# Inverse deviations of the routed tokens: square root and reciprocal against logarithm and exponential

## The chip, the cores and the metric

One core of one Trainium2 chip runs the whole kernel. The metric is the device time of one execution in microseconds (us), given as the median of three runs. The engines are PE (TensorE), ACT (ScalarE), DVE (VectorE), POOL (GpSimd) and SP (the engine that issues most transfers).

## The reference, cut to what matters

3125 nodes with 256 features pass through a graph layer (53125 edges), a linear attention layer, and then a mixture of experts: 8 experts, 2 per token. The change touches only the layer norm ahead of the experts and what is handed on from it.

```python
def _layernorm(x, axis=-1, eps=1e-05):
    m = jnp.mean(x, axis=axis, keepdims=True)
    v = jnp.var(x, axis=axis, keepdims=True)
    return (x - m) / jnp.sqrt(v + eps)

xn = _layernorm(x)
x = x + gnn(xn, src, dst) + mix(xn)
x = x + ffn(_layernorm(x)[None])[0]     # tokens = _layernorm(x)

# in ffn, for each token:
probs = softmax(tokens @ router_w.T)
rw, re = top_k(probs, 2); rw = rw / rw.sum(-1)
out = tokens
for e in range(8):
    h = gelu(tokens @ w1[e] + b1[e]); y = h @ w2[e] + b2[e]
    out = out + combine[:, e:e + 1] * y
```

The kernel sends only the normalized token through the experts. So that the un-normalized x can be added at the end, each token's row also carries its mean (column MEAN) and one plus its deviation (column SPAN): x + tokens = tokens * (deviation + 1) + mean.

## The kernel before, in words

The 3125 nodes are 25 tiles of 125 rows. The kernel runs in three stages. In the first (to about 262 us of the profiled span) nodes are normalized, the attention is computed, and edges are counted into adjacency blocks that PE multiplies. In the second, which I call routing, the tiles are taken in six groups `ROUT` of 2, 5, 5, 5, 5 and 3 tiles. In the third (from about 332 us) 62 chunks of 128 rows go through the experts' two matrix products.

The change lies in routing. Each engine has its own program, written out by hand, and semaphores order them. For a group g the steps are:

- PE `graph3(g)` (L1423) makes the last graph layer's output of the group.
- DVE `add_graph(g)` adds it to x (L1038), takes moments (L1045) and aggregates them (L1048), which leaves mean and variance in `rows[..., MEAN:SPAN+1]` and raises `var2_done`.
- ACT `token_scale(g)` (L668 to L677) waits for that, writes the square root of variance plus eps to `std2` (L673), and then overwrites SPAN with deviation plus one (L676).
- DVE `scale(g)` makes the reciprocal `rstd2` (L1057) and `shift2` = -mean * rstd2 (L1058).
- ACT `normalize_tokens(g)` (L683) applies scale and shift, one instruction per tile, and raises `tk_done` for each.
- PE `transpose_tokens(g)` (L1437) waits for `tk_done` of the whole group. ACT `copy_tokens(g)` (L693, L695) copies the transposed tokens out of the banks. PE `logits(g)` (L1448) multiplies them by the router's weights.
- DVE `choose(g)` (L1065 to L1083) takes the two best experts, ACT takes an exponential of the difference of their logits (L707), PE `positions(g)` (L1460, L1462) counts places in the experts' lists, and DVE `weigh(g)` (L1092 to L1103) makes weights and slots.
- POOL sends the group's tiles to their slots (L559), after `tk_done`, `span_done` and `slot_done`.

The groups are overlapped by the order of each program. ACT's loop for g is: `normalize_tokens(g+1)`, the exponential of g, `copy_tokens(g+1)`, `token_scale(g+2)`. DVE's is: `scale(g+1)`, `choose(g)`, `add_graph(g+2)`, `weigh(g)`. PE's loop, with the filler products `keep_clock` (L1194) that do no work but keep PE busy, is:

```python
            for g in range(NR):
                if g + 2 < NR:
                    graph3(g + 2)
                if g + 1 < NR:
                    pe.wait_ge(tkT_done, copies_to(g + 1))
                    keep_clock(m0, 8)
                    transpose_tokens(g + 1)
                positions(g)
                if g + 1 < NR:
                    pe.wait_ge(lg_read, g + 1)
                    keep_clock(lg_ps, 3)
                    logits(g + 1)
```

After the last group DVE works out the table of chunks (L1118 to L1153), and SP then loads the chunks of the third stage.

ACT evaluates its functions from tables. An ACT_TABLE_LOAD stands in its stream, under the line of the function that needs it, wherever the active table lacks that function.

Of the kernel before, what the change touches and what calls it, by code (L numbers as in the profile page):

```python
# [9 lines left out]
ACT = mybir.ActivationFunctionType  # L10
# [4 lines left out]
TP = 125  # L15
NT = N // TP
J = 5
# [12 lines left out]
TOKEN, NEXT, W_LOW, W_HIGH, MEAN, SPAN = range(D, D + 6)  # L30
# [11 lines left out]
ROUT = [(0, 2), (2, 7), (7, 12), (12, 17), (17, 22), (22, 25)]  # L42
NR = len(ROUT)
# [14 lines left out]
def build(nc, a, out):  # L58
# [4 lines left out]
    with ExitStack() as ctx:  # L63
        def sb(name, shape, dt=F32):
            return ctx.enter_context(nc.sbuf_tensor(name, shape, dt))

        def sem(name):
            return ctx.enter_context(nc.semaphore(name))
# [14 lines left out]
        class Region:  # L83
# [15 lines left out]
        rows = sb("rows", [P, NT, ROW])  # L99
# [92 lines left out]
        ones = sb("ones", [TP, P])  # L192
# [7 lines left out]
        epsc = sb("epsc", [TP, 1])  # L200
# [41 lines left out]
        qn = sb("qn", [P, 2, 2 * TP])  # L242

        stats2 = sb("stats2", [TP, 2, J, 6])
        std2 = sb("std2", [TP, 2, J])
        rstd2 = sb("rstd2", [TP, 2, J])
        shift2 = sb("shift2", [TP, 2, J])
        lg = sb("lg", [TP, J, NX])
# [46 lines left out]
        h1_done, h1_dve, g2_ready, h2_act, h2_dve = map(sem, ("h1_done", "h1_dve", "g2_ready", "h2_act", "h2_dve"))  # L295
        w_in, b2_in, b2_step, b2_done, rows_set, null_set, nulls_stored = map(sem, (
            "w_in", "b2_in", "b2_step", "b2_done", "rows_set", "null_set", "nulls_stored"))
        g3_ready, x2_done, stats2_done, var2_done, std2_done, shift2_done, tk_done = map(sem, (
            "g3_ready", "x2_done", "stats2_done", "var2_done", "std2_done", "shift2_done", "tk_done"))
        t3_ready, tkT_done, lg_ready, lg_read, diff_done, ex_done, oh_done, pos_ready, pos_read = map(sem, (  # L300
            "t3_ready", "tkT_done", "lg_ready", "lg_read", "diff_done", "ex_done", "oh_done", "pos_ready", "pos_read"))
        slot_done, cum_done, table_done = map(sem, (
# [1 line left out]
        span_done, top_done, slot_known = sem("span_done"), sem("top_done"), sem("slot_known")  # L304
# [291 lines left out]
        def _(act):  # L596
# [43 lines left out]
            for t in range(NT):  # L640
                if t in (1, 8):
                    lo, hi = (J, 3 * J) if t == 1 else (3 * J, NT)
# [25 lines left out]
            def token_scale(g):  # L668
                lo, hi = ROUT[g]
                act.wait_ge(var2_done, g + 1)  # L670
                if g >= 2:
                    act.wait_ge(shift2_done, g - 1)
                nc.scalar.activation(std2[:, g % 2, 0:hi - lo], rows[0:TP, lo:hi, SPAN], ACT.Sqrt, bias=epsc[:]  # L673
                                     ).then_inc(std2_done, 1)
                act.wait_ge(std2_done, g + 1)
                nc.scalar.activation(rows[0:TP, lo:hi, SPAN], std2[:, g % 2, 0:hi - lo], ACT.Identity,  # L676
                                     bias=ones[:, 0:1]).then_inc(span_done, 1)  # L677

            def normalize_tokens(g):
                lo, hi = ROUT[g]  # L680
# [5 lines left out]
            def copy_tokens(g):  # L686
# [7 lines left out]
                if n == J:  # L694
                    nc.scalar.copy(tkT[:, g % 2, :, 4 * TP:5 * TP], h0[:, 0:CB].rearrange("p (k n) -> p k n", k=2)  # L695
                                   ).then_inc(tkT_done, 1)

            token_scale(0)
            normalize_tokens(0)
            copy_tokens(0)  # L700
            token_scale(1)
            for g in range(NR):
                n = ROUT[g][1] - ROUT[g][0]
# [41 lines left out]
        def _(dve):  # L745
            step = [0]

            def link(ins):
                step[0] += 1
                ins.then_inc(dve_step, 1)  # L750
                dve.wait_ge(dve_step, step[0])
# [274 lines left out]
            def chain(ins):  # L1026
                link(ins)

            def add_graph(g):
                lo, hi = ROUT[g]  # L1030
                if g >= 3:
                    dve.wait_ge(tk_done, ROUT[g - 3][1])
                dve.wait_ge(g3_ready, hi)
                for j in range(min(3, hi - lo)):
                    both = hi - lo > j + 3
                    end = j + 4 if both else j + 1
                    got = (y0, y1, spare)[j][0:TP, 0:(1 + both) * D].rearrange("p (j d) -> p j d", d=D)
                    nc.vector.scalar_tensor_tensor(x2[:, g % 3, j:end:3, :], got, 0.0, xb[:, lo + j:lo + end:3, :],  # L1038
                                                   ALU.max, ALU.add).then_inc(x2_done, 1 + both)
                known = lo  # L1040
                for t in sorted(range(lo, hi), key=lambda t: ((t - lo) % 3, t)):
                    if t - lo < 3:
                        known += 2 if t + 3 < hi else 1
                        dve.wait_ge(x2_done, known)
                    nc.vector.bn_stats(stats2[:, g % 2, t - lo, :], x2[:, g % 3, t - lo, :]).then_inc(stats2_done, 1)  # L1045
                dve.wait_ge(stats2_done, hi)
                for j in range(hi - lo):
                    last = nc.vector.bn_aggr(rows[0:TP, lo + j, MEAN:SPAN + 1], stats2[:, g % 2, j, :])  # L1048
                last.then_inc(var2_done, 1)

            def scale(g):
                lo, hi = ROUT[g]
                n = hi - lo
                dve.wait_ge(std2_done, g + 1)
                if g >= 2:
                    dve.wait_ge(tk_done, ROUT[g - 2][1])
                chain(nc.vector.reciprocal(rstd2[:, g % 2, 0:n], std2[:, g % 2, 0:n]))  # L1057
                nc.vector.scalar_tensor_tensor(shift2[:, g % 2, 0:n], rows[0:TP, lo:hi, MEAN], -1.0, rstd2[:, g % 2, 0:n],  # L1058
                                               ALU.mult, ALU.mult).then_inc(shift2_done, 1)

            def choose(g):
                lo, hi = ROUT[g]
                n = hi - lo
                dve.wait_ge(lg_ready, g + 1)
                nc.vector.tensor_copy(lg[:, 0:n, :].rearrange("p j x -> p (j x)"), lg_ps[0:TP, 0:n * NX]  # L1065
                                      ).then_inc(lg_read, 1)
                dve.wait_ge(lg_read, g + 1)
                for j in range(n):
                    last = nc.vector.max(top[:, j, :], lg[:, j, :])
                chain(last)  # L1070
                for j in range(n):
                    last = nc.vector.max_index(top_at[:, j, :], top[:, j, :], lg[:, j, :])
                last.then_inc(top_done, 1)
                nc.vector.tensor_tensor(ex[:, 0:n], top[:, 0:n, 1], top[:, 0:n, 0], ALU.subtract).then_inc(diff_done, 1)
                dve.wait_ge(top_done, g + 1)
                for r2, (order, pick) in enumerate(((ALU.is_lt, ALU.min), (ALU.is_gt, ALU.max))):
                    nc.vector.tensor_tensor(first[:, 0:n, r2], top_at[:, 0:n, 0], top_at[:, 0:n, 1], order)
                    last = nc.vector.tensor_tensor(role[:, 0:n, r2], top_at[:, 0:n, 0], top_at[:, 0:n, 1], pick)
                chain(last)
                for r2 in range(2):  # L1080
                    last = nc.vector.tensor_tensor(oh[:, lo:hi, r2, :], iota_x[:, 0:n, :],
                                                   role[:, 0:n, r2:r2 + 1].to_broadcast([TP, n, NX]), ALU.is_equal)
                last.then_inc(oh_done, 1)  # L1083
# [4 lines left out]
            def weigh(g):  # L1088
                lo, hi = ROUT[g]
                n = hi - lo  # L1090
                dve.wait_ge(ex_done, g + 1)
                nc.vector.tensor_tensor(first[:, 0:n, :], first[:, 0:n, :], of_both(ex, n), ALU.max)  # L1092
                chain(nc.vector.tensor_scalar(exs[:, 0:n], ex[:, 0:n], 1.0, None, ALU.add))
                chain(nc.vector.reciprocal(exs[:, 0:n], exs[:, 0:n]))
                nc.vector.tensor_tensor(rows[0:TP, lo:hi, W_LOW:W_HIGH + 1], first[:, 0:n, :], of_both(exs, n), ALU.mult)
                dve.wait_ge(pos_ready, g + 1)
                nc.vector.tensor_tensor(place[:, 0:n, :], pos_from(lo, hi).rearrange("p (j n) -> p j n", n=2 * NX),
                                        oh[:, lo:hi].rearrange("p j r x -> p j (r x)"), ALU.mult).then_inc(pos_read, 1)
                dve.wait_ge(pos_read, g + 1)
                nc.vector.tensor_reduce(slot_f[:, 0:n], place[:, 0:n, 0:NX], AX_X, ALU.add).then_inc(slot_known, 1)  # L1100
                nc.vector.tensor_reduce(rows[0:TP, lo:hi, NEXT], place[:, 0:n, NX:2 * NX], AX_X, ALU.add)
                dve.wait_ge(slot_known, g + 1)
                nc.vector.tensor_copy(slot_i[0:TP, lo:hi, 0], slot_f[:, 0:n]).then_inc(slot_done, 1)  # L1103
# [2 lines left out]
            nc.vector.tensor_scalar(cum[:], base[:], 1.0 / TP, None, ALU.mult).then_inc(cum_done, 1)  # L1106
            add_graph(0)
            scale(0)
            add_graph(1)
            for g in range(NR):  # L1110
                if g + 1 < NR:
                    scale(g + 1)
                choose(g)
                if g + 2 < NR:
                    add_graph(g + 2)
                weigh(g)
# [442 lines left out]
```

## Time and profile before

| | us |
|---|---|
| median of three runs | 474.47 |
| lowest, highest run | 474.03, 477.58 |
| the profiled execution's own time | 479.72 |
| its span, first to last instruction | 478.0 |
| first stage, to | about 262 |
| routing, from and to | about 262 to 332 |
| third stage, from | about 332 |
| PE, DVE, ACT, POOL busy in the span | 435.7, 312.7, 283.2, 175.2 |

The profile is of one execution, 5.25 us longer than the median of the runs. All rows come from it. Their times are counted from the first instruction.

### The profile page before, as it was taken

Reading aid. Unit: us, or ns where it says so; the run is one execution under the profiler, and the core shown is the slowest. Engines: PE = TensorE matmul, PEld = TensorE weight load, DVE = VectorE, ACT = ScalarE, POOL = GpSimd, SP = SyncE. Lnnn points to the kernel's source line nnn. Section 1 sums busy time; section 2 is a strip of 40 time slices with the busy share of each in tenths; the row PEclk is TensorE's granted clock in tenths of the full one; section 3 lists DMA queues with packets and bytes.
Section 4 is the critical chain, followed back from the end, with each engine's and each line's share of the span. In section 5 each row is a group of like instructions: output and inputs, shape, how many; then the busy total and the mean of one; then the engine's idle time right before and its main releaser. Section 6 shows DMA issues by size and latency. Waiting matters only on the chain.

```text
span 478.0 us, 9967 instructions
## 1 busy us (share of the span) xinstructions
PE 435.7 (91%) x3245; PEld 324.2 (68%) x3254; DVE 312.7 (65%) x860; ACT 283.2 (59%) x630; POOL 175.2 (37%) x236
## 2 busy tenths in 40 slices
PE   1899899989999999999998989877899999999990
PEld 0687687866666666555665656553899999889890
DVE  3687959867777777777751787638466666666660
ACT  1657554766767767677772686751676776444440
POOL 5045686454111111111110014455244454544442
PEclk9899999999999999999999979787999999999996
DMA  8827111936789799877776001112466565566640
GB/s 213 182 63 239 41 27 25 331 70 122 119 161 161 150 181 184 183 145 138 142 122 123 1 25 58 57 67 90 115 196 193 175 186 160 152 190 171 186 132 2
DMA packets 111458, 63.05 MB, mean 132 GB/s; under 512 B 87753, under 2 KB 101970, under 8 KB 111406
## 3 DMA queue, kind: packets, MB, share of 16 engines
q1 hardware_dynamic: 104222, 47.11, 44.3%
q0 software_dynamic: 6368, 14.44, 8.9%
q10 hardware_dynamic: 816, 0.85, 0.7%
q8 instruction: 27, 0.44, 0.4%
q14 instruction: 25, 0.20, 0.1%
HBM read 22.96 MB, written 21.44 MB: 93 GB/s over the span
## 4 chain that ended last, share of the span: by engine, by line
PE 71%; DMA 7%; DVE 6%; ACT 6%; issue 3%; POOL 2%; SPq 1%; another core or an unknown queue 1%; POOLq 0%; DVEq 0%; ACTq 0%
PE bank L1300 12%; PE bank L1505 10%; PE bank L1516 10%; PE bank L1251 9%; PE bank L1331 4%; PE bank L1218 4%; PE bank L1227 4%; DMA region_a<-region_a 3%; PE bank L1494 3%; PE bank L1234 3%; DMA rows<-in_x 2%; PE bank L1194 2%; PE bank L1448 2%; PE bank L1311 2%; ACT rows L683 1%
## 5 line engine op out<-in xcount | busy, mean ns | idle before, releaser
L636 ACT CAST region_a<-bank 128x500 bf16<-128x500 f32 (+1 forms) x175 | 112.1, 667 | 46.2 <-PE bank L1251 42.0
L1300 PE MATMUL bank<-region_a,region_z 125*64 125x500 bf16 (+1 forms) x525 | 69.8, 361 | 2.5 <-DMA region_a<-region_a 2.5
L1251 PEld LDWEIGHTS bank<-region_a 128*128 128x128 bf16 x625 | 41.2, 101 | 42.7 <-issue 31.0
L1251 PE MATMUL bank<-region_a 128*128 128x125 bf16 x625 | 64.8, 220 | 1.7 <-ACT region_a L636 1.4
L1505 PE MATMUL bank<-region_a,region_c 128*128 128x128 f32 x496 | 65.8, 275 | 0.3 <-issue 0.3
L1516 PE MATMUL bank<-region_c,region_a 128*128 128x256 f32 x248 | 63.7, 379 | 0.0
L1505 PEld LDWEIGHTS bank<-region_a,region_c 128*128 128x128 f32 x496 | 60.2, 191 | 0.9 <-issue 0.5
L725 ACT ACTIVATE region_a<-bank,region_c 128x128 f32<-128x128 f32 x124 | 38.9, 365 | 33.7 <-PE bank L1505 33.2
L530 POOL COPY wide<-den 125x256 f32<-125x256 f32 x25 | 12.9, 514 | 119.5 <-DVE den L948 119.5
L1163 DVE COPY region_c<-region_w 128x1026 f32 x62 | 43.2, 697 | 16.2 <-issue 15.3
L572 POOL DMA_INDIRECT xs_next<-region_a x31 | 31.4, 1014 | 43.2 <-DVE region_a L1174 42.5
L887 DVE TENSOR_TENSOR region_a<-iota,locs 128x3200 bf16<-128x3200 bf16 x25 | 45.9, 1835 | 0.0
L1516 PEld LDWEIGHTS bank<-region_c,region_a 128*128 128x128 f32 x248 | 42.3, 190 | 4.0
L881 DVE TENSOR_TENSOR region_a<-iota,keys 128x3150 bf16<-128x3150 bf16 x25 | 44.8, 1790 | 0.0
L578 POOL DMA_INDIRECT out<-region_a x31 | 32.0, 1034 | 32.9 <-DVE region_a L1174 31.0
L559 POOL DMA_INDIRECT xs<-rows,slot_i x25 | 24.5, 979 | 51.1 <-DVE slot_i L1103 45.0
L717 ACT COPY region_a<-bank 128x256 f32<-128x256 f32 x62 | 23.1, 373 | 30.2 <-PE bank L1494 23.2
L1300 PEld LDWEIGHTS bank<-region_a,region_z 125*64 125x64 bf16 x525 | 24.4, 108 | 21.4 <-DMA region_a<-region_a 3.0
L1218 PE MATMUL bank<-wzkv,region_a 128*125 128x320 f32 x100 | 32.4, 447 | 0.0
L1171 DVE CAST region_a<-region_a 128x1 int32<-128x1 f32 x62 | 9.5, 154 | 33.9 <-PE bank L1516 29.2
L1194 PE MATMUL bank<-zeros,ones 128*128 128x512 bf16 x98 | 29.4, 443 | 1.5 <-issue 1.1
L1227 PEld LDWEIGHTS bank<-region_a,wq 128*128 128x128 f32 x200 | 27.9, 202 | 4.4 <-issue 0.6
(219 smaller groups left out, 756.1 us busy)
## 6 DMA issues: line engine op xcount, KB each, us to landing
region_a<-xs_next SPq DMA_DIRECT2D x31, 259.0 KB
region_w<-in_w SPq DMA_DIRECT2D x4, 1024.0 KB, 9.7
region_a<-xs SPq DMA_DIRECT2D x31, 131.0 KB
rows<-in_x SPq DMA_DIRECT2D x5, 560.0 KB
xs_next<-null SPq DMA_DIRECT2D x8, 259.0 KB, 2.7
xs_next<-null SPq DMA_DIRECT2D x1, 1554.0 KB, 10.7
xs<-null SPq DMA_DIRECT2D x8, 131.0 KB, 2.3
xs<-null SPq DMA_DIRECT2D x1, 786.0 KB, 7.2
```

The costliest lines, as they stand in the source:

```text
L636: nc.scalar.copy(to, count_bank(n)[:, 0:w * TP].rearrange("p (c t u) -> p c t u", c=w, t=NT)).then_inc(adj_done, 1)
L725: last = nc.scalar.activation(hT[:, c % 2, f * P:(f + 1) * P], hid_ps[c % 2][:, f * P:(f + 1) * P], ACT.Gelu, bias=wc[:, c % 3, 4 * D + f: ...
L881: nc.vector.tensor_tensor(koh[:, t % 2, :, :].rearrange("p c (m u) -> p c m u", u=2), counting(KW), columns(keys, t, KW), ALU.is_equal).th ...
L887: nc.vector.tensor_tensor(loh[:, t % 2, :, :].rearrange("p c (m u) -> p c m u", u=2), counting(P), columns(locs, t, P), ALU.is_equal).then ...
L1163: nc.vector.tensor_copy(wc[:, c % 3, :].rearrange("p (a f) -> p a f", a=1), w_all[:, bass.ds(e, 1), :])
L1194: nc.tensor.matmul(ps[:], ones16[:], zeros[:], start=True, stop=True)
L1218: last = nc.tensor.matmul((y0, y1)[s][0:TP, 0:H1 + D], xnT[:, s, k, :], wzkv[:, k, 0:H1 + D], start=(k == 0), stop=(k == 1))
L1227: last = nc.tensor.matmul((h0, h1)[s][:, c * TP:(c + 1) * TP], wq[:, k, c * P:(c + 1) * P], xnT[:, s, k, :], start=(k == 0), stop=(k == 1))
L1251: last = nc.tensor.matmul(count_bank(n)[:, (c - lo) * TP:(c - lo + 1) * TP], loh[:, t % 2, c, :], koh[:, t % 2, c, 0:TP], start=True, stop ...
L1300: last = nc.tensor.matmul(block_out(b), zparts[:, t, part, :], adjT[0:TP, t % 2, lo:hi, 0:TP], start=False, stop=False, skip_group_check=True)
L1505: last = nc.tensor.matmul(hid_ps[c % 2][:, f * P:(f + 1) * P], wc[:, c % 3, k * D + f * P:k * D + (f + 1) * P], xT[:, c % 2, k * P:(k + 1) ...
L1516: last = nc.tensor.matmul(y_ps[c % 2][:, 0:D], hT[:, c % 2, f * P:(f + 1) * P], wc[:, c % 3, (2 + f) * D:(3 + f) * D], start=False, stop=( ...
```

## The change

ACT takes the logarithm of variance plus eps (into a new tile `log2`), and from it the exponential of -0.5 times that, which is the inverse deviation `rstd2` itself. DVE no longer makes `rstd2` in `scale(g)`. ACT no longer writes SPAN. A new DVE step `restore_scale(g)` takes the reciprocal of `rstd2`, which is the deviation, and writes it plus one to SPAN. It runs right after `scale(0)` for group 0 and after `choose(g-1)` for the others. The waits that protect the buffers follow.

```diff
@@ ACT
             def token_scale(g):
                 lo, hi = ROUT[g]
                 act.wait_ge(var2_done, g + 1)
+                nc.scalar.activation(log2[:, g % 2, 0:hi - lo], rows[0:TP, lo:hi, SPAN], ACT.Ln, bias=epsc[:]
+                                     ).then_inc(log2_done, 1)
+                act.wait_ge(log2_done, g + 1)
                 if g >= 2:
-                    act.wait_ge(shift2_done, g - 1)
-                nc.scalar.activation(std2[:, g % 2, 0:hi - lo], rows[0:TP, lo:hi, SPAN], ACT.Sqrt, bias=epsc[:]
-                                     ).then_inc(std2_done, 1)
-                act.wait_ge(std2_done, g + 1)
-                nc.scalar.activation(rows[0:TP, lo:hi, SPAN], std2[:, g % 2, 0:hi - lo], ACT.Identity,
-                                     bias=ones[:, 0:1]).then_inc(span_done, 1)
+                    act.wait_ge(span_done, g - 1)
+                    act.wait_ge(tk_done, ROUT[g - 2][1])
+                nc.scalar.activation(rstd2[:, g % 2, 0:hi - lo], log2[:, g % 2, 0:hi - lo], ACT.Exp, scale=-0.5
+                                     ).then_inc(rstd2_done, 1)
@@ DVE
             def scale(g):
                 lo, hi = ROUT[g]
                 n = hi - lo
-                dve.wait_ge(std2_done, g + 1)
+                dve.wait_ge(rstd2_done, g + 1)
                 if g >= 2:
                     dve.wait_ge(tk_done, ROUT[g - 2][1])
-                chain(nc.vector.reciprocal(rstd2[:, g % 2, 0:n], std2[:, g % 2, 0:n]))
                 nc.vector.scalar_tensor_tensor(shift2[:, g % 2, 0:n], rows[0:TP, lo:hi, MEAN], -1.0, rstd2[:, g % 2, 0:n],
                                                ALU.mult, ALU.mult).then_inc(shift2_done, 1)
+
+            def restore_scale(g):
+                lo, hi = ROUT[g]
+                chain(nc.vector.reciprocal(std2[:, 0:hi - lo], rstd2[:, g % 2, 0:hi - lo]))
+                nc.vector.tensor_scalar(rows[0:TP, lo:hi, SPAN], std2[:, 0:hi - lo], 1.0, None, ALU.add
+                                        ).then_inc(span_done, 1)
@@ DVE, the loop
             add_graph(0)
             scale(0)
+            restore_scale(0)
             add_graph(1)
             for g in range(NR):
                 if g + 1 < NR:
                     scale(g + 1)
                 choose(g)
+                if g + 1 < NR:
+                    restore_scale(g + 1)
                 if g + 2 < NR:
                     add_graph(g + 2)
                 weigh(g)
```

## Rows read from the trace of the kernel before

**Rows 1.** Instruction groups of ACT: count, busy us, mean ns, idle before

```profile
L673 ACT ACT_TABLE_LOAD x5 | 6.4, 1283 | 0.1
L707 ACT ACT_TABLE_LOAD x5 | 6.4, 1283 | 0.1
...
L673 ACT ACTIVATE std<-rows,epsc 125x5 f32<-125x5 f32 (+2 forms) x6 | 1.8, 301 | 1.6 <-DVE rows L1048 1.5
...
L707 ACT ACTIVATE ex<-ex 125x5 f32<-125x5 f32 (+2 forms) x6 | 1.2, 206 | 4.0 <-DVE ex L1074 3.9
```

**Rows 2.** Chain that ended last, in routing: start us, us, what

```profile
276.89 1.28 ACT L707
...
290.70 1.28 ACT L673
...
295.33 1.28 ACT L707
296.63 0.21 ACT ex L707
296.84 2.05 another core or an unknown queue
...
310.91 1.28 ACT L673
...
314.54 1.28 ACT L707
```

**Rows 3.** Timeline of ACT in routing: start us, us, instructions, idle before

```profile
268.76 0.30 ACT L673 ACTIVATE std<-rows,epsc 125x2 f32<-125x2 f32 x1 [0.33 <-DVE rows L1048]
...
273.55 0.30 ACT L673 ACTIVATE std<-rows,epsc 125x5 f32<-125x5 f32 x1 [1.19 <-DVE rows L1048]
...
274.31 2.57 ACT L683 ACTIVATE rows<-region_a,shift,rstd 125x256 f32<-125x256 f32 x5
...
278.32 1.05 ACT L693 COPY region_a<-bank 128x500 f32<-128x500 f32 x2
...
292.75 2.57 ACT L683 ACTIVATE rows<-region_a,shift,rstd 125x256 f32<-125x256 f32 x5
...
312.94 1.58 ACT L683 ACTIVATE rows<-region_a,shift,rstd 125x256 f32<-125x256 f32 x3
...
318.67 0.85 ACT L693 COPY region_a<-bank 128x375 f32<-128x375 f32 x2 [2.63 <-remote]
```

**Rows 4.** Timeline of PE in routing, the same columns

```profile
277.02 1.26 PE L1437 MATMUL bank<-ident,rows 125*128 125x125 f32 x10 [0.63 <-ACT rows L683]
...
282.40 2.07 PE L1423 MATMUL bank<-w3g,region_z 32*125 32x256 f32 x10
284.80 3.19 PE L1194 MATMUL bank<-zeros,ones 128*128 128x512 bf16 x7 [0.33 <-issue]
...
293.01 1.13 PE L1423 MATMUL bank<-w3g,region_z 32*125 32x256 f32 x10
294.30 1.67 PE L1194 MATMUL bank<-zeros,ones 128*128 128x512 bf16 x7 [0.16 <-issue]
295.81 1.23 PE L1437 MATMUL bank<-ident,rows 125*128 125x125 f32 x10
...
314.87 0.81 PE L1437 MATMUL bank<-ident,rows 125*128 125x125 f32 x6
```

**Rows 5.** Timeline of DVE in routing, the same columns

```profile
269.78 1.62 DVE L1038 SCALAR_TENSOR_TENSOR region_a<-bank,rows 125x512 f32<-125x512 f32 x3 [0.33 <-PE bank L1423]
...
292.33 0.19 DVE L1057 RECIPROCAL rstd<-std 125x5 f32<-125x5 f32 x1 [1.60 <-ACT std L673]
292.55 0.16 DVE L1058 SCALAR_TENSOR_TENSOR shift<-rows,rstd 125x5 f32<-125x5 f32 x1
...
298.77 0.45 DVE L1048 BATCH_NORM_AGGREGATE rows<-stats 125x2 f32<-125x6 f32 x5 [0.21 <-DVE stats L1045]
...
318.71 0.24 DVE L1097 TENSOR_TENSOR place<-bank,region_a 125x80 f32<-125x80 f32 x1 [1.13 <-remote]
```

More of the change, by code:

```diff
@@ L244, in build @@
         stats2 = sb("stats2", [TP, 2, J, 6])
-        std2 = sb("std2", [TP, 2, J])
+        log2 = sb("log2", [TP, 2, J])
+        std2 = sb("std2", [TP, J])
         rstd2 = sb("rstd2", [TP, 2, J])
@@ L297, in build @@
             "w_in", "b2_in", "b2_step", "b2_done", "rows_set", "null_set", "nulls_stored"))
-        g3_ready, x2_done, stats2_done, var2_done, std2_done, shift2_done, tk_done = map(sem, (
-            "g3_ready", "x2_done", "stats2_done", "var2_done", "std2_done", "shift2_done", "tk_done"))
+        g3_ready, x2_done, stats2_done, var2_done, log2_done, rstd2_done, shift2_done, tk_done = map(sem, (
+            "g3_ready", "x2_done", "stats2_done", "var2_done", "log2_done", "rstd2_done", "shift2_done", "tk_done"))
         t3_ready, tkT_done, lg_ready, lg_read, diff_done, ex_done, oh_done, pos_ready, pos_read = map(sem, (
```

## The prediction

> **What bounds the kernel now.** I read the groups of ACT instructions first, since the change swaps functions there. Ten table loads stand in routing: five under the square root (L673) and five under the exponential of the logits (L707), 1283 ns each [rows 1]. They alternate because `token_scale(g+2)` and the exponential of g alternate. That is 12.8 us of ACT time in a stage of about 70 us.
>
> The question is how much of it is on the path. The chain that ended last says: five of the ten, 5 x 1.28 = 6.4 us [rows 2]. But that chain enters ACT twice through a piece named "another core or an unknown queue", after an exponential has ended and before the next copy starts: 2.05 us at 296.84 [rows 2], and again ahead of the copy at 318.67, which waited 2.63 us [rows 3]. So the chain doesn't really know who released the copy. I therefore went to the timelines and set the two candidates side by side, group by group.
>
> `transpose_tokens(g)` on PE needs two things: PE's own earlier work (logits, `graph3`, eight fillers), and the end of ACT's normalization. Group 3: ACT's normalization starts at 292.75 and lasts 2.57, so it ends at 295.32 [rows 3]. PE's fillers end at 294.30 + 1.67 = 295.97, and the transposes are recorded from 295.81 [rows 4]. PE is last, by 0.5 us. Group 5: normalization ends at 312.94 + 1.58 = 314.52 [rows 3], the transposes start at 314.87 [rows 4]. PE is last by 0.35 us. [...] Only group 1 is set by ACT: PE sat idle 0.63 us until L683 had ended [rows 4], and ahead of that ACT had waited 1.19 us for DVE's moments [rows 3].
>
> [...]
>
> **The change, part by part.** *The small instructions on ACT.* Before, where the square root needs no load, it takes 273.55 to 274.31 from its start to the start of the normalization, 0.76 us [rows 3]: square root 0.30, reciprocal 0.19, shift 0.17, and three hand-overs of about 0.03 [rows 1, 5]. After: logarithm, exponential, shift. No row shows a logarithm. I bound it by the two activations on this tile shape: 0.206 (no bias tile, L707) and 0.301 (bias tile, L673) [rows 1]. It has the same bias tile as the square root, so I take 0.30. The exponential has no bias tile, so I take 0.21. Sum 0.30 + 0.21 + 0.17 + three hand-overs = 0.77. The path through the scale is as long as before; the range of this term is 0.1 either way, for each group where it binds, which is one.
>
> *The SPAN write on ACT* (L676, six of about 0.30) leaves ACT. It was covered: it ran while DVE made reciprocal and shift. Worth nothing.
>
> *DVE.* `scale(g)` loses a reciprocal of 0.19 plus a hand-over. `restore_scale(g)` adds a reciprocal of 0.19, a hand-over, and an addition of about 0.17 (nearest row, the shift) [rows 5], 0.4 in all. For groups 1 to 5 it stands after `choose(g-1)` and ahead of `add_graph(g+1)`. What is late next is the variance of the group after, and ACT doesn't use it at once: moments for group 4 end at 298.77 + 0.45 = 299.22 [rows 5], while ACT comes to them only after the copies that start behind the unknown piece, at 296.84 + 2.05 = 298.9 [rows 2]. So 0.2 net is hidden there. It also stands ahead of `weigh`, whose product with the positions waited 1.13 us anyway in the group where slots are latest [rows 5]. For group 0 it stands ahead of `add_graph(1)`, which started at 269.78 and had waited for PE [rows 5]. After the change DVE is free about 269.93 (square root at 268.76 [rows 3], 0.77 to the normalization, and 0.4). That is 0.15 us later, and this is group 1's path. If that cover is worth nothing at all the term is 0.4; if PE is late it is 0.
>
> *New waits.* ACT's exponential of group g waits for `restore_scale(g-2)` and for the normalization of g-2. Both precede by a whole round of the loops. Queued behind it on ACT would be normalization and copies, but nothing waits. POOL's sends need `span_done`, now from DVE, and this comes well ahead of `slot_done` of the same group. Nothing.
>
> *The table loads.* This is the large term and it depends on which tables the compiler picks. Loads stand only under the two functions [rows 1]; copies and normalizations run under either table. No row shows a logarithm. If one table serves logarithm and exponential, all ten loads in routing go, or nine. Then ACT reaches the end of normalization about 1.3 us earlier in groups 2 to 5. [...] In group 1 the exponential of group 0 loses its load at 276.89 [rows 2], but the copies behind it started at 278.32 [rows 3], and the transposes they read ended at 277.02 + 1.26 = 278.28 [rows 4]. [...]
>
> [...]
>
> Sum for the likeliest case: loads 0, small instructions 0.0, group 0's restore +0.15. Against the profiled execution: 479.72 (span 478.0 and 1.72 around it) + 0.15 = 479.9. That execution is 5.25 us above the median, so against the runs: 474.47 + 0.15 = 474.6.
>
> **The rivals.** *Two tables instead of one (slower).* If the compiler gives the logarithm one table and the exponential another, each `token_scale` has two loads, one ahead of the logarithm and one between it and the exponential, and the exponential of the logits none. The count is then 12 in place of 10, and the second load lies inside the chain. Group 0: inverse deviation 1.3 later, so DVE ends shift and restore at about 271.2 and `add_graph(1)` starts 1.4 later. Group 1 has its own second load, 1.3, so the normalization ends 2.7 later, and PE was waiting for it. Groups 3 and 5: ACT 1.3 later less the slack of 0.5 and 0.35, together 1.7. Groups 2 and 4: covered at half clock, about 0.8 each at full clock. Sum +4.4 to +6.0, so 478.9 to 480.5. It decides once the second load exceeds PE's slack, which is 0.35 to 0.5 us at full clock. For it: nothing in the rows says that the two functions share a table. [...]
>
> *The chain is right and the ACT path binds (faster).* If the two unexplained pieces follow ACT rather than PE, groups 3 and 5 gain two loads each: 4 x 1.28 = 5.1, so 469.4. For it: the chain. Against it: in group 5 the copy on ACT (318.67) and the product on DVE (318.71) were released together, both "remote" [rows 3, 5], and the two wait for PE alone.
>
> *The clock moves.* PE's clock halves in two rounds of routing. Such a stretch costs (3.19 - 1.67) + (2.07 - 1.13) = 2.5 us and something on the transposes [rows 4]. A shift in PE's pauses could add one or remove one: 472.1 or 477.1. Nothing in the change aims at it.
>
> **How the numbers follow.** One table and no effect, 474.6: 0.50, own range 473.5 to 475.8. Two tables: 0.30. ACT path binds: 0.10. Clock: 0.10, half on each side. About 1% (4.7 us) is what a measurement of this kernel can tell from no change. The two-table case passes 479.2 in about two thirds of its spread, 0.20, with 0.03 for the clock on top of it. The ACT case passes 469.8 in most of its spread, 0.08. That leaves 0.69 within 1%. The range goes from 472.0 (a stretch at half clock gone) to 480.5 (two tables at full clock); it leaves out the 0.10 of the ACT case and a little above.
>
> **What would show it.** Right: no table load at L673's successor, nor at L707, in routing; ACT idle ahead of L693 longer by 1.3 us or more in groups 2 to 5, released by PE; the transposes of each group as late as before against the copies of the group ahead. Wrong: loads between logarithm and exponential, and PE idle ahead of the transposes; or copies of groups 3 and 5 that come earlier by two loads. If the transposes start earlier than the fillers' end before, my reading of PE as last is wrong.

## The result and the profile after

The change makes the kernel slower by 0.9%: 480.1 us median (477.55 to 482.66) against 476.78 of the kernel before (471.94 to 478.89), 17 runs each, ratio 1.0089 with a 95% interval of 1.0065 to 1.0113. Ratios are estimated over the single runs, without executions more than 1.5% above the fastest of their kernel; the two medians alone give 1.0070. Run again on two chips, the change stood at 1.0131 (1.0089 to 1.0172) and 1.0121 (1.0075 to 1.0168). I had forecast no effect. The slower rival, two tables in place of one, came true, at 3.3 us by these medians and 4.2 us by the ratio, where I had worked out 4.4 to 6.0.

The groups of ACT instructions of the kernel after (line, count, busy us, mean ns, idle before) answer to [rows 1]:

```profile
L672 ACT ACT_TABLE_LOAD x6 | 7.7, 1283 | 0.1
L678 ACT ACT_TABLE_LOAD x6 | 7.7, 1283 | 0.1
...
L672 ACT ACTIVATE log<-rows,epsc 125x5 f32<-125x5 f32 (+2 forms) x6 | 1.8, 301 | 0.5 <-DVE rows L1050 0.3
...
L678 ACT ACTIVATE rstd<-log 125x5 f32<-125x5 f32 (+2 forms) x6 | 1.2, 206 | 0.1
L709 ACT ACTIVATE ex<-ex 125x5 f32<-125x5 f32 (+2 forms) x6 | 1.2, 193 | 2.7 <-DVE ex L1081 2.7
```

Twelve loads in place of ten. The exponential of the logits (L709) has none any more, but each inverse deviation has two, one ahead of the logarithm (L672) and one between it and the exponential (L678). The timeline of ACT of the kernel after shows the pair in group 1, where [rows 3] has 0.76 us from the square root's start to the normalization:

```profile
272.90 1.28 ACT L672 ACT_TABLE_LOAD   x1
274.29 0.30 ACT L672 ACTIVATE log<-rows,epsc 125x5 f32<-125x5 f32 x1
274.60 1.28 ACT L678 ACT_TABLE_LOAD   x1
275.90 0.21 ACT L678 ACTIVATE rstd<-log 125x5 f32<-125x5 f32 x1
276.34 2.56 ACT L685 ACTIVATE rows<-region_a,shift,rstd 125x256 f32<-125x256 f32 x5 [0.23 <-DVE shift L1059]
```

From logarithm to normalization it is 276.34 - 274.29 = 2.05 us, 1.29 more than before. All six transposes of PE (timeline of the kernel after; the last bracket is PE's idle time and who ended it) answer to [rows 4]:

```profile
271.60 0.62 PE L1447 MATMUL bank<-ident,rows 125*128 125x125 f32 x4 [0.78 <-ACT rows L685]
...
279.05 1.26 PE L1447 MATMUL bank<-ident,rows 125*128 125x125 f32 x10 [2.12 <-ACT rows L685]
...
287.88 1.82 PE L1447 MATMUL bank<-ident,rows 125*128 125x125 f32 x10
...
297.20 1.26 PE L1447 MATMUL bank<-ident,rows 125*128 125x125 f32 x10 [0.78 <-ACT rows L685]
...
306.23 1.23 PE L1447 MATMUL bank<-ident,rows 125*128 125x125 f32 x10
...
313.96 0.83 PE L1447 MATMUL bank<-ident,rows 125*128 125x125 f32 x6 [0.94 <-ACT rows L685]
```

Here PE waits for the normalization of groups 0, 1, 3 and 5 and not of 2 and 4, whose fillers ran in part at half clock (2.80 and 3.09 us for the seven recorded, in place of 1.67). That is the rival's pattern: a normalization 2.7 us later in group 1, 0.8 and 0.95 us lost in groups 3 and 5, nothing at half clock. The early part repeats exactly. In the three profiles of the changed kernel (`after`, `after_again`, `after_c`) the copies of group 1 start 17.85 to 17.86 us after the first activation at the head of routing, in the kernel before 15.39 us (278.32 - 262.93): 2.46 us are lost by then. First the first activation of the kernel before, then that of the kernel after with its copies of group 1:

```profile
262.93 1.06 ACT L658 ACTIVATE region_a<-bank 128x500 f32<-128x500 f32 x2 [8.97 <-PE bank L1189]
```

```profile
262.49 1.07 ACT L659 ACTIVATE region_a<-bank 128x500 f32<-128x500 f32 x2 [10.63 <-PE bank L1199]
...
280.34 1.05 ACT L695 COPY region_a<-bank 128x500 f32<-128x500 f32 x2 [1.35 <-PE bank L1447]
```

The late part does not repeat. PE waits for ACT in groups 3 and 5 in `after`, in group 4 alone in `after_again` (1.21 us) and in group 5 alone in `after_c` (0.94 us). The late groups without such a wait ran their fillers at half clock, or partly so (2.7 to 3.4 us for the seven or eight that are recorded, in place of 1.7 to 1.9). So which late groups pay differs from one execution to the next.

**A trap in the two profiles.** The profiled execution of the kernel after took 478.36 us (span 476.6), less than the 479.72 of the one before, though the medians say the reverse. Two things differ. The first is the granted clock. These are stretches of 20 us, the last of them reaching into the third stage, of the kernel before and then of the kernel after (us; busy us of the engines; granted clock, then DMA share and GB/s at the end):

```profile
280.00:300.00 20.00, 17.71 (x111) 12.63 (x112) 14.48 (x94) 13.92 (x26) 6.89 (x7) 0.83 0.14 48
300.00:320.00 20.00, 16.16 (x96) 11.36 (x99) 10.12 (x78) 13.36 (x25) 9.69 (x10) 0.80 0.18 67
320.00:340.00 20.00, 15.90 (x76) 9.71 (x78) 11.52 (x56) 4.80 (x13) 7.91 (x8) 0.77 0.31 94
```

```profile
280.00:300.00 20.00, 18.17 (x122) 12.83 (x122) 15.38 (x98) 15.57 (x30) 6.90 (x7) 0.91 0.14 47
300.00:320.00 20.00, 16.37 (x113) 11.48 (x116) 13.84 (x115) 14.08 (x26) 12.19 (x13) 0.91 0.23 82
320.00:340.00 20.00, 15.47 (x73) 9.87 (x71) 10.36 (x36) 4.77 (x14) 6.10 (x7) 0.83 0.32 95
```

Read in steps of 1 us from 280 to 340, the granted clock is 1.00 in 33 steps of the kernel before and 0.50 in 22, and lies between the two in the other five, each beside a change of level; in the kernel after it is 41, 11 and eight. So one minus the clock, doubled, is the share of the stretch at half clock: before 24 us of these 60, after 14. It needn't be the change's doing. The 17 executions of the changed kernel range from 477.55 us at a mean clock of 0.975 to 482.66 at 0.959, and a profile catches one of them. The kernel before shows the same on the four chips of the experiments: a straight line through its executions gives 2.2, 2.6, 3.0 and 3.3 us more for 0.01 less mean clock.

The second is a wait of ACT that the profile puts down to no engine of this core ("remote"). In group 3 of the kernel before, the transposes are recorded to 295.81 + 1.23 = 297.04 and the copies that read them start 1.92 us later. In the kernel after it is 298.55 - (297.20 + 1.26) = 0.09 us. These are the two copies, before and after:

```profile
298.96 1.05 ACT L693 COPY region_a<-bank 128x500 f32<-128x500 f32 x2 [2.12 <-remote]
```

```profile
298.55 1.05 ACT L695 COPY region_a<-bank 128x500 f32<-128x500 f32 x2 [1.39 <-PE bank L1447]
```

In group 5 it is 318.67 - (314.87 + 0.81) = 2.99 us before [rows 3, 4] and 0.09 after. The two pieces are 4.9 us of waiting in the profiled execution of the kernel before, as much as the whole effect of the change. So I read profiles here for the order of events in a group, and took times from the medians of runs that stand side by side.

### The profile page after: what moved, and what is told of

It reads as the page before. It is cut to its first block, busy times and chain, and to the rows that moved or that the text cites. A ratio compares the mean times of both kernels' runs of the same rounds, so it can differ in the third digit from the quotient of the medians.

```text
span 476.6 us, 9975 instructions
## 1 busy us (share of the span) xinstructions
PE 432.7 (91%) x3245; PEld 321.1 (67%) x3254; DVE 312.7 (66%) x866; ACT 284.7 (60%) x632; POOL 174.6 (37%) x236
## 4 chain that ended last, share of the span: by engine, by line
PE 67%; DMA 9%; DVE 8%; ACT 5%; POOL 4%; issue 3%; SPq 1%; POOLq 0%; DVEq 0%; ACTq 0%
PE bank L1310 12%; PE bank L1515 10%; PE bank L1261 9%; PE bank L1526 9%; PE bank L1341 4%; PE bank L1228 4%; PE bank L1237 3%; DMA region_a<-region_a 3%; PE bank L1504 3%; POOL xs L560 2%; DMA rows<-in_x 2%; PE bank L1244 2%; DMA region_a<-xs_next 2%; PE bank L1321 2%; DMA out<-region_a 1%
## 5 line engine op out<-in xcount | busy, mean ns | idle before, releaser
L1310 PE MATMUL bank<-region_a,region_z 125*64 125x500 bf16 (+1 forms) x525 | 71.1, 367 | 2.5 <-DMA region_a<-region_a 2.5
L1515 PE MATMUL bank<-region_a,region_c 128*128 128x128 f32 x496 | 66.9, 278 | 0.0
L1515 PEld LDWEIGHTS bank<-region_a,region_c 128*128 128x128 f32 x496 | 61.5, 195 | 0.2
L1204 PE MATMUL bank<-zeros,ones 128*128 128x512 bf16 x98 | 28.3, 431 | 2.2 <-DVE expert_i L1163 1.1
```

Of the source, the lines that this page charges most:

```text
L1310: last = nc.tensor.matmul(block_out(b), zparts[:, t, part, :], adjT[0:TP, t % 2, lo:hi, 0:TP], start=False, stop=False, skip_group_check=True)
L1515: last = nc.tensor.matmul(hid_ps[c % 2][:, f * P:(f + 1) * P], wc[:, c % 3, k * D + f * P:k * D + (f + 1) * P], xT[:, c % 2, k * P:(k + 1) ...
```

## The experiments

The versions ran on four chips, each with its own runs of the kernel before beside them. That kernel's median was 480.22, 479.95, 474.48 and 480.59 us there, so times are compared only on one chip, and ratios are always to the kernel before on the same chip. Line numbers shift by a few with the edits.

### One table for both functions

The only edit to the changed kernel is one explicit table load ahead of group 0:

```diff
+            def load_table(which):
+                nc.scalar.add_instruction(mybir.InstLoadActFuncSet(
+                    name=nc.get_next_instruction_name(), act_func_set_id=which, ins=[], outs=[]))
...
+            load_table(6)
             token_scale(0)
```

That table 6 holds logarithm and exponential is read from this run. Behind the one load (L670, at 268.67 us, 1283 ns) six logarithms (L676) and twelve exponentials (six under L682, six under L714) run without another. The next load stands at 321.75 us (L741), behind the last exponential, for the third stage's function. So it is one load in routing in place of twelve.

> The changed kernel with one instruction added: ahead of the scale of group 0, ACT loads the table that holds logarithm and exponential together. The 12 loads of 1.28 us in routing become one. Theory 1 (the loss is the second load inside the chain, and beyond that PE and its fillers are last): the loss goes and no gain comes, about the time of the kernel before, ratio 1.000, at most 0.15 us over it. Theory 2 (ACT's chain sets every group, so each load counts): 10 loads of the kernel before go as well, at least 5 us faster than before, ratio 0.989 or less. Theory 3 (the loss comes from the DVE reciprocal and addition and the added hand-overs): it stays at about 1.009.

Measured: 481.81 us, ratio 1.0037 (1.0008 to 1.0066). The timeline of ACT in its group 3 shows the load-free chain, and how long ACT then waits ahead of the copies:

```profile
292.11 0.33 ACT L676 ACTIVATE log<-rows,epsc 125x5 f32<-125x5 f32 x1
292.46 0.21 ACT L682 ACTIVATE rstd<-log 125x5 f32<-125x5 f32 x1
292.90 2.57 ACT L689 ACTIVATE rows<-region_a,shift,rstd 125x256 f32<-125x256 f32 x5 [0.23 <-DVE shift L1064]
296.26 0.21 ACT L714 ACTIVATE ex<-ex 125x5 f32<-125x5 f32 x1 [0.79 <-DVE ex L1086]
300.32 1.05 ACT L699 COPY region_a<-bank 128x500 f32<-128x500 f32 x2 [3.85 <-remote]
```

ACT was idle 2.12 us there in the kernel before (the line at 298.96 above); now it is 3.85, and 0.79 more ahead of the exponential. The loads' time turned into waiting. The interval is just above 1.000, so I ran this kernel on two more chips (the third and the fourth).

> one_table once more, beside the next three. Theory 1 (only the tables matter): within 0.15 us of the kernel before but for the clock, 1.000 to 1.003. Theory 5 (something else of the change costs about 1.5 us, beyond the tables): 1.0037 again, with the mean clock as before's.

> one_table a third time. Theory 1: 1.000 to 1.003. Theory 5: 1.004.

Measured: 475.87 us, ratio 1.0014 (0.9979 to 1.0049), and 482.09 us, 1.0007 (0.9967 to 1.0046). Beside the last stood the changed kernel itself.

> The changed kernel beside one_table_c on one chip. Theory 1: 4.4 to 6 us above one_table_c, ratio 1.009 to 1.013 against the kernel before.

Measured: 486.88 us, 1.0121. The difference on one chip is 486.88 - 482.09 = 4.8 us, at mean clocks of 0.967 and 0.966, which is inside what the rival gave (4.4 to 6.0). An earlier repeat agrees:

> The changed kernel as it is, to have it beside the next three on one chip. All theories: 1.006 to 1.012 against the kernel before, about 4 us. Theory 4 (each execution's time follows how long PE runs at half clock, and the variants differ in that too): mean granted clock of its executions at least as high as before's, so that at equal clock the loss is larger than 4 us.

Measured: 485.65 us, 1.0131 (1.0089 to 1.0172), 5.7 us over its kernel before. Its mean clock was 0.966 against 0.970 there, so "at least as high as before's" was wrong; by that chip's line (2.6 us for 0.01) about 1 us of the 5.7 goes with the clock, an estimate.

### One more load on the old chain

```diff
             def token_scale(g):
                 lo, hi = ROUT[g]
+                load_table(0)
                 act.wait_ge(var2_done, g + 1)
```

> The kernel before, with one more table load ahead of each square root (square root and reciprocal stay as they were). Theory 1: one more load of 1.28 us in the chain of each group costs what the change cost. Group 0 about 1, group 1 about 1.5 to 2.7, groups 3 and 5 about 0.8 each, groups 2 and 4 nothing at half clock: 3 to 6 us, ratio 1.006 to 1.012. Theory 2: 5 to 6 loads of 1.28 on the path, 6.4 to 7.7 us, ratio 1.014 or more. Theory 3: no change from before, 1.000.

Measured: 484.35 us, ratio 1.0108 (1.0073 to 1.0142), 4.1 us over its kernel before by the medians and 5.2 by the ratio. Square root, reciprocal and SPAN write are those of the kernel before, and the loss of the change is there all the same. Table 0 doesn't serve the square root: the trace has six of the added loads (L669) and, right behind each, one under the square root (L678), 1283 ns every one. In group 1, whose square root needed no load before, that makes two more loads and not one, as in the change (two in `token_scale(1)`, none before). PE's waits for the normalization, from the timeline of this kernel (groups 0, 1, 3, 5), are nearly those of the change:

```profile
272.35 0.62 PE L1442 MATMUL bank<-ident,rows 125*128 125x125 f32 x4 [0.44 <-ACT rows L688]
279.71 2.07 PE L1442 MATMUL bank<-ident,rows 125*128 125x125 f32 x10 [2.04 <-ACT rows L688]
...
298.84 1.26 PE L1442 MATMUL bank<-ident,rows 125*128 125x125 f32 x10 [0.77 <-ACT rows L688]
...
318.49 0.83 PE L1442 MATMUL bank<-ident,rows 125*128 125x125 f32 x6 [0.93 <-ACT rows L688]
```

### Which groups pay

`two_first` loads table 6 at group 2 only, and groups 0 and 1 have two tables: its trace shows two loads under the logarithm (L678), two under the exponential (L684), the added one (L670) at 284.62 us, and none after it in routing. `two_last` has table 6 in groups 0 and 1 and loads table 5 from group 2 on. Table 5 serves the logarithm and not the exponential: the trace shows five added loads (L670, the first of them of table 6), four under the exponential (L686, groups 2 to 5) and none under the logarithm (L680).

```diff
@@ two_first
+                if g == 2:
+                    load_table(6)
                 act.wait_ge(var2_done, g + 1)
@@ two_last
+                if g == 0:
+                    load_table(6)
+                if g >= 2:
+                    load_table(5)
                 act.wait_ge(var2_done, g + 1)
```

> The changed kernel with the table of both functions loaded ahead of the logarithm of group 2: groups 0 and 1 have two tables as in the change (4 loads), groups 2 to 5 have one. Theory 1 (the loss is where PE has no slack): groups 0 and 1 carry 2.7 of the 4.4 us, so 2.7 us over one_table, and 1.7 us under the change. If every second load counts alike: 2 of 6, 1.4 us over one_table.

Measured: 483.79 us, ratio 1.0088 (1.0055 to 1.0121).

> The changed kernel with the table of both functions loaded ahead of group 0, and the separate tables again from group 2 on (logarithm's table ahead of each logarithm, the exponential's ahead of each exponential). Theory 1: groups 3 and 5 lose 0.8 and 0.9, groups 2 and 4 nothing at half clock and 0.8 each at full clock: 1.7 to 3.3 us over one_table. PE waits for L689's counterpart ahead of the transposes of groups 3 and 5, and not in group 1.

Measured: 482.89 us, ratio 1.0060 (1.0033 to 1.0088). Against the kernel before on this chip (479.95): 3.8 us with the second load in two groups, 2.9 with it in four, 5.7 for all six. By the medians the two early groups cost more than the four late ones, as PE's slack has it, though the two intervals overlap; a third of 5.7, as an even share would be, is 1.9. `two_first` is 1.9 us under the changed kernel, where I expected 1.7; the sizes over `one_table` can't be had, since it didn't run on this chip. PE's waits for ACT part in the same way. First `two_first` (groups 0 and 1 wait 0.78 and 2.12, the rest not), then `two_last` (group 1 waits 0.64, as in [rows 4], groups 3 and 5 wait 0.79 and 0.94):

```profile
273.81 0.62 PE L1453 MATMUL bank<-ident,rows 125*128 125x125 f32 x4 [0.78 <-ACT rows L691]
281.26 1.97 PE L1453 MATMUL bank<-ident,rows 125*128 125x125 f32 x10 [2.12 <-ACT rows L691]
```

```profile
275.04 1.26 PE L1455 MATMUL bank<-ident,rows 125*128 125x125 f32 x10 [0.64 <-ACT rows L693]
...
293.19 1.26 PE L1455 MATMUL bank<-ident,rows 125*128 125x125 f32 x10 [0.79 <-ACT rows L693]
...
313.28 0.83 PE L1455 MATMUL bank<-ident,rows 125*128 125x125 f32 x6 [0.94 <-ACT rows L693]
```

### Are the old ten loads worth anything

This version leaves the square root out. An identity stands in its place, so its output isn't that of the layer, but nothing else in the order of work changes, and the trace shows no table load in routing (the next, L734, comes at 321.62 us, behind the last exponential).

```diff
-                nc.scalar.activation(std2[...], rows[0:TP, lo:hi, SPAN], ACT.Sqrt, bias=epsc[:]
+                nc.scalar.activation(std2[...], rows[0:TP, lo:hi, SPAN], ACT.Identity, bias=epsc[:]
```

> The kernel before with the square root left out (an identity with the same bias in its place, so the scale is that of the variance), which needs no table of its own: the ten loads in routing go and nothing else changes. Theory 1 (PE is last): 1.000, at most 0.3 us faster. Theory 2 (the chain of waits is right): 5 us faster, 0.989. Theory 4 (ACT being earlier changes when PE's clock falls): slower, 1.003 to 1.005, as one_table and sqrt_ahead were, with a lower mean clock.

Measured: 480.4 us, ratio 1.0017 (0.9986 to 1.0047). Ten loads gone, 12.8 us of ACT, and nothing gained: the interval leaves room for 0.7 us at most, so 5 us faster is excluded. So the five loads that the chain of waits named [rows 2] were not on the path. This was the faster rival, and it falls.

The same question with the count of loads kept: the square root's table taken ahead, where ACT waits for PE. Table 3 serves the square root: behind the four added loads (L669) the square roots of groups 2 to 5 (L677) have none of their own, and only that of group 0 has one.

```diff
                 nc.scalar.activation(ex[:, 0:n], ex[:, 0:n], ACT.Exp).then_inc(ex_done, 1)
+                if g + 2 < NR:
+                    load_table(3)
```

> The kernel before, with the square root's table loaded right after the exponential of the logits, ahead of the copies of the transposed tokens, where ACT waits for PE, in place of after them. The count of loads is as before (10), four of them leave the stretch between copies and square root. Theory 1: PE is last, so nothing is gained, ratio 0.998 to 1.001. Theory 2: four loads leave the path, 5 us faster, ratio 0.989.

Measured: 482.01 us, ratio 1.0042 (1.0015 to 1.0070). Slower, which neither theory had. One place shows in the timelines of PE and ACT. In group 1 there is no wait to hide in: the transposes end at 277.96 + 1.26 = 279.22, and the copies start only when the load ends, 1.4 us later.

```profile
277.96 1.26 PE L1443 MATMUL bank<-ident,rows 125*128 125x125 f32 x10 [0.63 <-ACT rows L687]
...
279.34 1.28 ACT L669 ACT_TABLE_LOAD   x1
280.64 1.05 ACT L697 COPY region_a<-bank 128x500 f32<-128x500 f32 x2
```

[rows 3] and [rows 4] had shown it: copies at 278.32, right behind the transposes' end at 278.28. I had moved a load past them without looking. Without that one load:

```diff
-                if g + 2 < NR:
+                if g >= 1 and g + 2 < NR:
                     load_table(3)
```

> sqrt_ahead without the load between the exponential of group 0 and the copies of group 1, which stood on the path there (group 1's copies came at 16.77 us after the stage's start in place of 15.39). Three loads are still taken ahead where ACT waits for PE. If that one load was the whole loss of sqrt_ahead: ratio 0.999 to 1.001. Theory 4 (ACT being earlier in itself makes PE's clock worse): 1.004 again. Theory 2: 3.8 us faster, 0.992.

Measured: 476.24 us, ratio 1.0030 (0.9993 to 1.0066). The interval reaches 1.000, so it can't be told from no change, and the point is 0.3% above it. Its interval overlaps that of `sqrt_ahead` too, so the times don't tell the two versions apart. That the one load was the loss is supported by the trace (group 1's copies are back at 15.38 us after the first activation of routing, from 16.77) and not shown by the time. A gain of 0.8% is excluded again.

### The DVE step

`one_table` without reciprocal and addition of SPAN, the semaphore raised alone:

```diff
-                chain(nc.vector.reciprocal(std2[:, 0:hi - lo], rstd2[:, g % 2, 0:hi - lo]))
-                nc.vector.tensor_scalar(rows[0:TP, lo:hi, SPAN], std2[:, 0:hi - lo], 1.0, None, ALU.add
-                                        ).then_inc(span_done, 1)
+                dve.sem_inc(span_done, 1)
```

> one_table with the DVE reciprocal and addition of the SPAN column left out (the column keeps the variance, so what the experts' rows carry is not the deviation; only the semaphore is raised). Theory 1: the same as one_table within what can be told, at most 0.15 us faster. Theory 5 with the DVE step as the cost: back at 1.000 while one_table stays at 1.003 to 1.004.

Measured: 474.71 us, ratio 1.0022 (0.9986 to 1.0059), beside 1.0014 for `one_table_b` on the same chip. The DVE step costs nothing that can be measured.

### Fewer fillers

If PE and its fillers are last, taking fillers away should pay, and more so where ACT has no loads.

```diff
                 if g + 1 < NR:
                     pe.wait_ge(tkT_done, copies_to(g + 1))
-                    keep_clock(m0, 8)
+                    keep_clock(m0, 4)
```

> one_table with four fillers in place of eight ahead of the transposes of groups 1 to 5. Theory 1: PE's own work is what is last in groups 2 to 5, and without table loads ACT is 1.6 us ahead of it, so four fillers of 0.21 us (0.43 at half clock) come off each: 3.4 us faster than one_table, more at half clock, if PE's clock holds. If the clock falls instead, it gives back 2.5 us for each round at half clock. Theory 2: PE isn't last and the fillers are free, the same as one_table.

Measured: 479.06 us, ratio 0.9976 (0.9943 to 1.0009), 2.8 us under one_table on the same chip. Then the kernel before, with the same edit:

> The kernel before with four fillers in place of eight ahead of the transposes, to see whether one_fill4's gain needs the single table. Theory 1: with its table loads ACT has 0.35 to 0.5 us of slack in groups 3 and 5 at full clock and 3.3 at half clock, so less comes off than in one_fill4: 0.4 twice and up to 1.7 twice, 1 to 4 us, ratio 0.992 to 0.998 if the clock holds. If fillers are free: 1.000.

Measured: 474.81 us, ratio 1.0000 (0.9964 to 1.0036). The two intervals overlap, so that fewer fillers pay more without loads is not shown. Its PE timeline does show PE waiting for ACT in groups 3 and 4, where it didn't in the kernel before:

```profile
293.09 1.26 PE L1437 MATMUL bank<-ident,rows 125*128 125x125 f32 x10 [0.35 <-ACT rows L683]
300.86 2.32 PE L1437 MATMUL bank<-ident,rows 125*128 125x125 f32 x10 [0.80 <-ACT rows L683]
```

> one_table with four fillers in place of eight, again. Theory 1: about 2 us under one_table_c with a wider spread than any other, since PE's pauses are longer and the clock falls more often: ratio 0.995 to 0.999. If its first result was the chip's doing: the same as one_table_c.

> one_table with six fillers. Theory 1: two fillers of 0.21 us in four groups come off, 1.7 us under one_table_c, with the clock less disturbed than with four: 0.996 to 0.999. If only the clock matters: as one_table_c.

Measured: 479.99 us, 0.9989 (0.9948 to 1.0029), and 480.88 us, 0.9988 (0.9953 to 1.0022), with one_table_c at 1.0007 beside them. The mean clock of `one_fill4_b` was 0.961 against 0.966 of one_table_c, and its runs spread from 476.39 to 485.48. `before_fill4` had 0.966 against 0.973 of its kernel before. What the fillers give thus seems to come back in part as lower clock (by that chip's line, 3.0 us for 0.01, about 2 us, an estimate), and no version with fewer of them is shown to beat the kernel before: all three intervals hold 1.000.

## Why the prediction was wrong

*What bounds the kernel.* Right on ACT, and shown: the transposes of groups 2 to 5 don't wait for it, the slack is 0.35 to 0.5 us at full clock (groups 3 and 5), and the chain of waits was wrong, since `no_loads` took ten loads away for nothing (1.0017). In groups 2 and 4 of the profile before the granted clock is 0.50 while the fillers run. Normalization ends at 281.72 + 2.57 = 284.29 and 302.36 + 2.56 = 304.92, and the transposes start at 287.79 and 307.74: PE is last by 3.5 and 2.8 us. ACT, then PE:

```profile
281.72 2.57 ACT L683 ACTIVATE rows<-region_a,shift,rstd 125x256 f32<-125x256 f32 x5
...
302.36 2.56 ACT L683 ACTIVATE rows<-region_a,shift,rstd 125x256 f32<-125x256 f32 x5
```

```profile
287.79 1.47 PE L1437 MATMUL bank<-ident,rows 125*128 125x125 f32 x10
...
307.74 1.73 PE L1437 MATMUL bank<-ident,rows 125*128 125x125 f32 x10
```

Group 1 is the one that ACT and DVE set. Incomplete on the rest: in groups 3 and 5 of the profile before, PE itself waited 2.07 and 2.30 us for copies that the "remote" piece held up, and my reading of PE as last leaves that out.

*The small instructions.* Right. The logarithm measured 301 ns (I took 0.30) and the exponential 206 (0.21). In `one_table` the normalization of group 1 starts 11.40 us after the first activation of routing (275.86 - 264.46), in the kernel before 11.38 (274.31 - 262.93).

*The DVE part.* Small, as I had it, but 0.15 too large. In the kernel after, reciprocal and addition of group 0 overlap the shift, and `add_graph(1)` starts 0.19 us after the shift's end, where I had added 0.4. In `one_table` it starts 6.85 us after the first activation (271.31 - 264.46), exactly as in the kernel before (269.78 - 262.93). `no_restore` shows no cost.

*The table loads.* This is the step that failed. I put half of the chance on one table for both functions and took that case's term of zero as the forecast. Both were my estimate: no row of before shows a table with both functions, nor which table a pair would be served from. A table with both does exist: `one_table` runs on it, with 18 logarithms and exponentials behind one load. But the compiler didn't pick it here. In the kernel after there are 12 loads for six pairs, one ahead of each logarithm and one ahead of the exponential behind it. "A table holds both" and "both will be served from that table" are two statements, and no row of before bore on either. I had this as the rival at 0.30, priced at 4.4 to 6.0 us; measured were 4.8 us against one_table on one chip, and 4.1 us with `extra_load`, which copies its mechanism onto the old kernel. The price was about right, group 1's 2.7 us (measured 2.46) above all. That groups 3 and 5 are the late ones that pay was in part luck: it held in one of three profiles. The 0.8 us each that this rival adds for groups 2 and 4 at full clock was an estimate too. The three profiles of the changed kernel show one such case, group 4 of `after_again`: fillers in 1.90 us, and PE waited 1.21. What was wrong is the term of zero in the sum. No run shows it for the change, and in its place stand 3.3 us by the medians of the first comparison, and 4.8 us against one_table on one chip. Where the loads do go, zero is within the interval: `no_loads`, with none of the ten, at 1.0017 (0.9986 to 1.0047).

*The sum and the range.* The time stands 3.3 us over the median before by the 17 runs, 4.2 us by the ratio. From the forecast of 474.6 it is 5.5 us away, and 2.3 of them are the starting point: the median of three runs, 474.47, lay that far under the 476.78 of 17. That 480.1 lies within 472.0 to 480.5 is no merit of the forecast, since the range's upper end came from this rival. The claim "no change" fails on the interval of 1.0065 to 1.0113.

*The clock.* Right that it moves single executions by several us, and too small a part of my reading of profiles: I compared a sum to one execution that, at 479.72 us and a clock of 0.962, was longer than all 17 runs (at most 478.89). That a shift in PE's pauses would add or remove a stretch at half clock was an estimate; no run shows what starts one.

*What stays open.* On three chips `one_table` stood at 1.0037, 1.0014 and 1.0007, and `no_loads`, `no_restore` and `sqrt_ahead2` at 1.0017 to 1.0030. Each alone but one holds 1.000 in its interval, yet none is under it. My working gives 0.15 us. Whether freeing ACT costs a further 0.2%, through when PE's clock falls, was not settled; the mean clock was below before's on the same chip in one_table (0.962 to 0.967), one_table_b (0.970 to 0.973) and no_loads (0.967 to 0.970), and above it in one_table_c (0.966 to 0.965). By the lines through the kernel before, these three differences go with 0.7 to 1.1 us (an estimate), about what stands over 1.000 in one_table_b and no_loads and more than half of it in one_table; that says nothing on which causes which. Nor do I know what the piece called "remote" ahead of the copies waits for. It is there with loads and without: in 12 of the 18 profiles some copy of groups 3 to 5 starts 0.4 to 3.8 us after the recorded end of its transposes. It is in none of the four profiles of the third chip, where the kernel before was fastest (474.48 us).

## What to carry to other kernels

Ask not only whether two functions can share a table but which table each will be served from, and if it matters load it by hand: one instruction here was worth 4.8 us. A load that moves from after a stage into its dependent chain is dearer than its count says: ten loads were free here (`no_loads`, 1.0017), and of twelve the three or four that PE couldn't cover cost 4 to 5 us. And before work is moved to where an engine waits, look for the round in which it doesn't wait.

## What I had not expected of the hardware

- A table load costs little beside its 1283 ns. In the kernel after, load at 274.60, exponential at 275.90: 1.30 us. In the 18 traces the next instruction of ACT starts 1.28 to 1.31 us after the start of the load for 195 of 240 loads. For the other 45 it starts 1.38 to 4.95 us after, and for 41 of them the trace records ACT as idle in between.
- Executions of one kernel on one chip spread by 3 to 11 us (`after_c`, `one_fill4`), in part with the mean granted clock (0.956 to 0.983 for the kernel before over the four chips), although 106 filler products stand around routing to keep PE busy.
- In the kernel after, the last work ahead of the third stage was not DVE's table of chunks but POOL's sends. The chain that ended last shows the last send, its landing, and SP's first step behind it:

```profile
324.53 1.15 POOL xs L560
325.68 0.30 issue
325.99 2.44 DMA xs<-rows,slot_i
328.51 0.48 SPq L404
```
